# A selective-scan block: where the turned B columns are made, and how two engines' diagonals are placed

## The chip, the cores and the metric

One NeuronCore of a Trainium2 chip runs the whole program. The metric is the device time in microseconds, the median of the runs; lower is better. Engines are named as in the profile: PE (TensorE; PEld is its weight load), DVE (VectorE), ACT (ScalarE), POOL (GpSimd), SP (SyncE, which here only issues DMAs).

## The reference, cut to what matters

The program is two residual layers on a batch of 8 images of 64 x 64 x 96. The change lies in the first one, a two-dimensional selective scan. For each of 8 images and 4 directions k (rows, columns, and both reversed) a sequence of 4096 positions is scanned in 192 channels with 16 states each:

```
dA = jnp.exp(dl[..., None] * A)
h = dA * h + (dl * ul)[..., None] * Bl[:, :, None, :]
y = jnp.einsum('bkdn,bkn->bkd', h, Cl)
```

Before it stand a group norm, a projection, a 3x3 depthwise convolution with SiLU and the projections to delta, B and C; behind it the sum of the four directions, a layer norm, a gate, a projection, and a second layer (an FFT-like upsampling, a squared two-matrix block and a low-pass).

## The kernel before

`scan_phase` is the long stage. A **step** is 1024 positions of one image, one direction and 96 of the 192 channels; there are 256 steps. Two steps (the two channel halves) share B, C and the projections and are called a **chunk** here: 128 chunks. A step has 12 **units**. A unit has 128 partitions (32 channels x 4 states) and 1024 positions; `ORDER = (2,2,2,0,3,3,3,0,1,1,1,0)` gives the group of 4 states of each of the 12 units. This text writes e0 to e11 for the units of a chunk's first step and o0 to o11 for those of its second.

Each unit goes through five engines' in-order lists:

- ACT `exp` (L841): E = exp(A * delta), three buffers (`NE`), so the exponential of a unit waits for the scan three units back. Each place of ACT's list makes the exponential two units ahead.
- PE `fill` (L642 or L677): the drive dl * u * B, spread over the partitions, into one of three PSUM slots (`NP = 3`). Where the group is 0 it is a plain spread of B (L642), multiplied by DVE (L742). In all others it is a product of the turned dl * u (`dluT`) with diagonal matrices of B: for groups 3 and 1 ACT makes these matrices (`diag`, L831, 64 small instructions a chunk), for group 2 (units 0 to 2 of a step) POOL makes them with two `affine_select` (`diagp`, L950). PE fills two units ahead of the unit in hand.
- DVE `scan` (L761): the recurrence, into four buffers H (`NH = 4`), so the scan of a unit waits for POOL's product four units back.
- POOL `weigh` (L961): HC = H * C, six buffers (`NHC`), so the product of a unit waits for the sum of the group of three that ended six units back or less.
- PE `sum_y` (L700, with L690 and L696 ahead of it in some directions): the sum over states, three units at a time in two halves. Its second half for units e6 to e8 stands in PE's list behind the fill of o2, and POOL's product of o0 waits for it.

Side jobs lie between the units: `x` (projection of the next chunk, L627, at e4), `dt` (two delta projections, L636, at e6 and e8; ACT's softplus of them, L807, at e8 and e10), `lt` (the transposes that give `dluT`, L657). On DVE the **split** (L736) stands behind the scan of e6 and waits for ACT's copies of the projection. POOL also makes dl * u (L942), once behind e7 and once behind o1.

Every unit and every side job takes the next of the three PSUM slots in one ring. A slot is free again when the job three places before it in the ring has been read:

```
place_of = {job: i for i, job in enumerate(ring)}
def bank(*job):
    return P[place_of[job] % NP]
```

B's columns must be turned (positions on the partitions) before the diagonals can be made. Before the change this is eight small matmuls (L652) at the head of `lt` of the next chunk, at o1, into spare columns of that job's slot (`BLT_AT`), copied by ACT to `blt` (L816) at o4. POOL's two selects stand behind its products of o5 and o7 (`POOL_AT = (6, 8)`). ACT's 64 diagonals are dealt over its places by `DIAGS`, whose first entry is the place of o3.

Order and names of the directions: k runs 0, 1, 3, 2 in even images and 2, 1, 3, 0 in odd ones. In the last two directions of an image earlier sums are added (L690), in direction 0 the skip term is (L696). Directions 1 and 3 read u in column order.

Of the kernel before, what the change touches and what calls it, by code (L numbers as in the profile page):

```python
# [16 lines left out]
C = 96  # L17
# [17 lines left out]
def namer(nc, ctx, prefix):  # L35

    def sem(name):
        return ctx.enter_context(nc.semaphore(f"{prefix}_{name}"))
    return sem
# [269 lines left out]
def scan_phase(nc, ctx, T, S):  # L309

    sem = namer(nc, ctx, "scan")
    NBLK = TC // 128
# [4 lines left out]
    KIND = tuple(DIRECT if g == GDIRECT else DIAGONAL for g in ORDER)  # L317
    ON = GDIAG + (GPOOL,)
    NDIAG = 4 * len(ON)
    DIAGS = (0, 0, 3, 8, 4, 3, 7, 17, 0, 0, 0, 11, 9, 2, 0, 0, 0, 0, 0, 0, 0, 0, 0, 0)  # L320
    DIAG_AT = 15
    PARTS = 2
    POOL_AT = (6, 8)
    NSLOT = 5
    NDUR = 3
    NP = 3
    BLT_AT = 416
    FILL_AHEAD = 2
    wx = T("wx", [C, NK, 2, 128])
    dtw = T("dtw", [C + NR, NK * ND], F32R)  # L330
# [4 lines left out]
    selt = T("selt", [C, NDIAG], F32R)  # L335
# [18 lines left out]
    blt = T("blt", [128, NBLK * NDIAG])  # L354
# [3 lines left out]
    sx = T("sx", [C + NR, 2, TC], F32R)  # L358
# [15 lines left out]
    NCHUNK = NSTEP // 2  # L374
    NUNIT = 12 * NSTEP
    NACT = 4 * NBLK * len(GDIAG)
# [8 lines left out]
    sx_split = sem("sx_split")  # L385
    dt_done = sem("dt_done")
    dl_made = sem("dl_made")
    dlu_made = sem("dlu_made")
    lt_done = sem("lt_done")
    lt_copied = sem("lt_copied")  # L390
    bt_copied = sem("bt_copied")
    diag_made = sem("diag_made")
    dl_out = [sem(f"dl_out{i}") for i in range(2)]
# [8 lines left out]
    pool_diag_made = sem("pool_diag_made")  # L402
    exp_done = sem("exp_done")
    scan_done = sem("scan_done")
# [36 lines left out]
    def slot(m, j):  # L441
        return (NJ * m + j) % NSLOT

    def loaded(m, j):
        return 64 * ((NJ * m + j) // NSLOT + 1)
# [39 lines left out]
    def side_jobs(n, x):  # L485
        c = n // 2 + 1
        jobs = []
        if n % 2 == 0:
            if x == 1:
                jobs += [("lt", n + 1)]  # L490
            if x == 4 and c < NCHUNK:
                jobs += [("x", c)]
            if x == 6 and c < NCHUNK:
                jobs += [("dt", 2 * c)]
            if x == 8 and c < NCHUNK:
                jobs += [("dt", 2 * c + 1)]
        elif x == 1 and c < NCHUNK:
            jobs += [("lt", 2 * c)]
        return jobs

    ring = [("x", 0), ("dt", 0), ("lt", 0), ("dt", 1)] + [("unit", un) for un in range(FILL_AHEAD)]
    for un in range(NUNIT):
        if un + FILL_AHEAD < NUNIT:
            ring += [("unit", un + FILL_AHEAD)]
        ring += side_jobs(*divmod(un, 12))
    place_of = {job: i for i, job in enumerate(ring)}
    released = {"unit": scan_done, "x": sx_split, "dt": dl_made, "lt": lt_copied}

    def bank(*job):
        return P[place_of[job] % NP]  # L510

    def bank_free(e, *job):
        i = place_of[job] - NP
        if i >= 0:
            e.wait_ge(released[ring[i][0]], ring[i][1] + 1)
# [97 lines left out]
    def tensor(e):  # L613
        def project(c, sub):
            b, k, ci, _ = steps[2 * c]
            t0 = t_of(k, ci) + sub * 512
            if sub == 0:
                bank_free(e, "x", c)
                rows_wait(e, 2 * c)
            o = bank("x", c)[:, sub * 512:(sub + 1) * 512]  # L620
            if k % 2:
                o = o.rearrange("p (w h) -> p h w", h=HW)
            for h in range(2):
                x = u[:, h, t0:t0 + 512]
                if k % 2:
                    x = u[:, h, :].rearrange("p (h w) -> p h w", w=HW)[:, :, t0 // HW:(t0 + 512) // HW]
                r = e.matmul(o, wx[:, k, h, :], x, start=h == 0, stop=h == 1)  # L627
            if sub:
                r.then_inc(x_done)

        def delta(m):
            b, k, ci, half = steps[m]
            bank_free(e, "dt", m)
            e.wait_ge(sx_split, m // 2 + 1)
            for sub in range(2):
                r = e.matmul(bank("dt", m)[0:C, sub * 512:(sub + 1) * 512], dtw[:, k * ND + half * C:k * ND + (half + 1) * C],  # L636
                             sx[:, m // 2 % 2, sub * 512:(sub + 1) * 512], start=True, stop=True)
            r.then_inc(dt_done)

        def spread(o, c):  # L640
# [2 lines left out]
                             start=True, stop=True)  # L643
            return r

        def turn(m):
            o = bank("lt", m)
            bank_free(e, "lt", m)
            if m % 2 == 0:
                e.wait_ge(sx_split, m // 2 + 1)  # L650
                for k in range(NBLK):
                    e.matmul(o[:, BLT_AT + NDIAG * k:BLT_AT + NDIAG * (k + 1)], sx[0:C, m // 2 % 2, k * 128:(k + 1) * 128],  # L652
                             selt[:], start=True, stop=True)
            e.wait_ge(dlu_made, m + 1)
            for k in range(NBLK):
                at = k // 4 * 512 + k % 4 * C
                r = e.transpose(o[:, at:at + C], dlu[:, k * 128:(k + 1) * 128], idn[0:C, 0:C])  # L657
            r.then_inc(lt_done)
# [49 lines left out]
        def side_job(name, n):  # L708
            if name == "x":
                project(n, 0)  # L710
                project(n, 1)
            elif name == "dt":
                delta(n)
            else:
                turn(n)

        side_job("x", 0)
        side_job("dt", 0)
        side_job("lt", 0)
        side_job("dt", 1)  # L720
        for un in range(FILL_AHEAD):
            fill(un)
        for un in range(NUNIT + 12):
            n, x = divmod(un, 12)
# [63 lines left out]
    def scalar(e):  # L788
# [9 lines left out]
        def delta(m):  # L798
            b, k, ci, half = steps[m]
            kk = k * 2 + half  # L800
            e.wait_ge(dt_done, m + 1)
            if m >= 2:
                e.wait_ge(dl_out[m % 2], 16 * (m // 2))
                e.wait_ge(dlu_made, m - 1)
            if m % 2 and m > 3:
                e.wait_ge(y_stored, 16 * (m - 3))
            e.activation(dl[m % 2], bank("dt", m)[0:C, :], ACT.Softplus, bias=dtb[:, kk:kk + 1]).then_inc(dl_made)  # L807

        def turn(m):
            o = bank("lt", m)  # L810
            e.wait_ge(lt_done, m + 1)
            if m % 2 == 0:
                if m:
                    e.wait_ge(diag_made, NACT * (m // 2))
                    e.wait_ge(pool_diag_made, PARTS * (m // 2))
                e.copy(blt[:].rearrange("p (n k) -> p k n", k=NBLK),  # L816
                       o[:, BLT_AT:BLT_AT + NBLK * NDIAG].rearrange("p (k n) -> p k n", n=NDIAG)).then_inc(bt_copied)
            if m >= 2:
                e.wait_ge(fill_done, last_of(m - 2, kinds=(DIAGONAL,)) + 1)
            e.copy(dluT[:, m % 2, :, :].rearrange("p (s k) c -> p s (k c)", s=2),  # L820
                   o.rearrange("p (s x) -> p s x", s=2)[:, :, 0:NBLK // 2 * C]).then_inc(lt_copied)
# [37 lines left out]
        def out_dl(m):  # L859
            if m >= 4:  # L860
                for j in range(NJ):
                    e.wait_ge(dlr_in[slot(m - 4, j)], loaded(m - 4, j))
            e.wait_ge(dl_made, m + 1)
            e.dma_start(S["dl"][m % 4], dl[m % 2]).then_inc(dl_out[m % 2], 16)
# [21 lines left out]
        out_bc(0)  # L886
        delta(0)
        out_dl(0)
        turn(0)
        delta(1)  # L890
        out_dl(1)
        e.wait_ge(a_made, 2)
        made = sum(DIAGS[:24 - DIAG_AT])
        diagonal(0, 0, min(made, 4 * NBLK))
# [3 lines left out]
        for un in range(NUNIT + 12):  # L898
            n, x = divmod(un, 12)
            c = n // 2 + 1  # L900
            exp(un + 2)
            if n < NSTEP and n % 2 == 0 and c < NCHUNK:
                if x == 6:
                    out_bc(c)
                if x == 9:
                    out_dl(2 * c)
                if x == 11:
                    out_dl(2 * c + 1)
            if x == 6 and n:
                store_y(n - 1)  # L910
            if un % 2 == 0 and has_carry(un - 1):
                carry(un - 1)
            if x == 5 and n:
                copy_y(n - 1)
            if n == NSTEP:
                continue
            if n % 2 == 0:
                if x == 2:
                    turn(n + 1)
                if x == 5 and c < NCHUNK:  # L920
                    project(c)
                if x == 8 and c < NCHUNK:
                    delta(2 * c)
                if x == 10 and c < NCHUNK:
                    delta(2 * c + 1)
            elif c < NCHUNK:
                if x == 4:
                    turn(2 * c)
            y = (12 * n + x - DIAG_AT) % 24
            d = c if 12 * (n % 2) + x >= DIAG_AT else c - 1  # L930
            if d < NCHUNK:
                diagonal(d, sum(DIAGS[:y]), DIAGS[y])

    def pool(e):
# [32 lines left out]
        for un in range(NUNIT + 1):  # L967
# [9 lines left out]
            else:  # L977
                if x == 2 and n + 2 < NSTEP:
                    delta(n + 2)
                if x in POOL_AT and c < NCHUNK:  # L980
                    diagonal(c, POOL_AT.index(x))

# [831 lines left out]
```

## Time and profile before

| | |
|---|---|
| median of 3 runs | 11437.5 us (11436.28 to 11439.11) |
| the profiled execution: its own time | 11433.25 us |
| its span, first to last instruction | 11431.5 us |
| stretch of the 128 splits | 624.7 to 9660.6 us |
| busy: PE, DVE, ACT, POOL | 10219.9, 9414.9, 8518.6, 9042.7 us |
| mean granted TensorE clock | 0.96 |

Shares are over the whole span; the scan is some 9100 us of it, and there the four engines are all busy for 82 to 92% of the time. So the shares don't name a bound, and the lists have to be read unit by unit.

### The profile page before, as it was taken

How to read it: one execution, taken by the hardware profiler on the slowest of the kernel's cores; microseconds unless marked ns; L12 is line 12 of the kernel's file. 1: busy time of each engine (PE TensorE's matmuls, PEld its weight loads, DVE VectorE, ACT ScalarE, POOL GpSimd, SP SyncE). 2: the span in 40 equal slices, each digit the busy share in tenths (PEclk: the TensorE clock that was granted, in tenths of full speed). 3: DMA queues.
4: the chain of work that ended last, by engine and by line, in shares of the span. 5: the costliest groups of instructions: out<-in, count | busy, mean ns of one | idle time of the engine just before them, and what ended most of it. 6: DMA issues, size and time to landing. Idle time of an engine off the chain costs nothing. (4 is left out here: it accounts for less than half of the span.)

```text
span 11431.5 us, 430806 instructions
## 1 busy us (share of the span) xinstructions
PE 10219.9 (89%) x185900; PEld 7314.0 (64%) x185900; DVE 9414.9 (82%) x5727; ACT 8518.6 (75%) x15618; POOL 9042.7 (79%) x3978
## 2 busy tenths in 40 slices
PE   8988898889988888899889888998898889799999
PEld 5656666666666666666666666666666666488888
DVE  7868888888888888888888888888888888555554
ACT  3478888888888888888888888888888888355454
POOL 1169999998999999999999999899999999634340
PEclk9989999999999999999999999999999999899999
DMA  3355666566656665666566656665666566322220
GB/s 100 111 156 155 163 168 167 155 163 163 167 156 163 168 163 155 163 167 164 155 163 168 165 156 163 166 166 154 163 171 166 154 164 165 94 70 68 66 68 13
DMA packets 547581, 1653.42 MB, mean 145 GB/s; under 512 B 148562, under 2 KB 149362, under 8 KB 542872
## 3 DMA queue, kind: packets, MB, share of 16 engines
q1 hardware_dynamic: 484248, 1416.10, 48.0%
q10 hardware_dynamic: 61440, 209.76, 6.1%
q8 instruction: 1471, 24.10, 0.9%
q14 instruction: 422, 3.46, 0.1%
HBM read 1251.98 MB, written 373.29 MB: 142 GB/s over the span
## 5 line engine op out<-in xcount | busy, mean ns | idle before, releaser
L961 POOL TENSOR_TENSOR HC<-H,crep 128x1024 f32<-128x1024 f32 x3072 | 7210.9, 2380 | 720.7 <-PE psum L700 681.7
L761 DVE TENSOR_TENSOR_SCAN H<-E,car,psum 128x1024 f32<-128x1024 f32 x2304 | 5282.4, 2334 | 535.7 <-PE psum L677 282.8
L841 ACT ACTIVATE E<-dlr,am 128x1024 f32<-128x1024 f32 x3072 | 3468.7, 1144 | 1335.2 <-DVE H L761 1311.3
L677 PE MATMUL psum<-diag,dluT 128*32 128x128 f32 x98304 | 3225.5, 275 | 360.1 <-DVE H L761 354.4
L677 PEld LDWEIGHTS psum<-diag,dluT 128*32 128x32 f32 x98304 | 2761.2, 110 | 1094.4 <-DVE H L761 702.8
L831 ACT ACTIVATE diag<-idn,blt 128x128 f32<-128x128 f32 x8192 | 2512.4, 389 | 42.5 <-PE psum L677 41.8
L677 PE MATMUL psum<-diagp,dluT 128*32 128x128 f32 x49152 | 1812.7, 302 | 656.8 <-POOL diagp L950 537.0
L677 PEld LDWEIGHTS psum<-diagp,dluT 128*32 128x32 f32 x49152 | 1636.5, 123 | 1027.7 <-issue 826.8
L700 PE MATMUL psum<-HC,sely 128*32 128x512 f32 x12288 | 2152.4, 598 | 22.5 <-POOL HC L961 21.3
L761 DVE TENSOR_TENSOR_SCAN H<-E,psum 128x1024 f32<-128x1024 f32 x768 | 1718.1, 2276 | 227.8 <-PE psum L677 84.9
L742 DVE TENSOR_TENSOR psum<-dur,psum 128x1024 f32<-128x1024 f32 x768 | 929.9, 1211 | 5.1 <-PE psum L642 1.1
L700 PEld LDWEIGHTS psum<-HC,sely 128*32 128x32 f32 x12288 | 431.4, 110 | 409.9 <-issue 365.6
L642 PE MATMUL psum<-sx,selb 96*128 96x512 f32 x1536 | 587.8, 463 | 7.1 <-DVE H L761 7.0
L642 PEld LDWEIGHTS psum<-sx,selb 96*128 96x128 f32 x1536 | 249.7, 189 | 431.8 <-DVE H L761 230.8
L1643 POOL TENSOR_TENSOR y<-y,tmp 96x1024 f32<-96x1024 f32 x60 | 189.6, 3210 | 417.0 <-DMA tmp<-scr_yk 417.0
L950 POOL TENSOR_SCALAR_AFFINE_SELECT diagp<-blt 128x2048 f32<-128x2048 f32 x256 | 514.9, 2012 | 2.0 <-ACT blt L816 2.0
L627 PE MATMUL psum<-u,wx 96*128 96x512 f32 x1024 | 475.7, 607 | 20.2 <-DVE dtw L773 20.2
L942 POOL TENSOR_TENSOR dlu<-dlt,u 96x1024 f32<-96x1024 f32 x128 | 340.0, 2656 | 175.4 <-ACT dlt L807 175.4
L1358 PEld LDWEIGHTS psum<-w2s,hs 128*100 128x100 f32 x4800 | 447.3, 168 | 15.2
L736 DVE TENSOR_TENSOR sx<-psum,sx 38x1024 fp32r<-38x1024 f32 x128 | 157.1, 1228 | 357.4 <-ACT sx L796 357.4
L1358 PE MATMUL psum<-w2s,hs 128*100 128x96 f32 x4800 | 447.8, 252 | 0.0
L45 PE MATMUL psum<-xp,wtap 96*96 96x512 f32 x1728 | 417.0, 400 | 0.0
(140 smaller groups left out, 9403.0 us busy)
## 6 DMA issues: line engine op xcount, KB each, us to landing
dur<-scr_dlu SPq DMA_DIRECT2D x3072, 128.0 KB, 3.5
dlr<-scr_dl SPq DMA_DIRECT2D x3072, 128.0 KB, 4.1
crep<-scr_bc SPq DMA_DIRECT2D x512, 256.0 KB, 4.9
crep<-scr_bc SPq DMA_DIRECT2D x1024, 128.0 KB, 3.0
scr_dlu<-dlu SPq DMA_DIRECT2D x256, 384.0 KB, 3.1
scr_yk<-yt ACTq DMA_DIRECT2D x256, 384.0 KB, 3.1
scr_dl<-dlt ACTq DMA_DIRECT2D x128, 384.0 KB, 4.0
scr_dl<-yt ACTq DMA_DIRECT2D x128, 384.0 KB, 4.6
```

The costliest lines, as they stand in the source:

```text
L45: r = e.matmul(o, w[p], x[q], start=first and i == 0, stop=last and i == 2)
L627: r = e.matmul(o, wx[:, k, h, :], x, start=h == 0, stop=h == 1)
L642: r = e.matmul(o[:, sub * 512:(sub + 1) * 512], selb[:], sx[0:C, c % 2, sub * 512:(sub + 1) * 512], start=True, stop=True)
L677: r = e.matmul(bank("unit", un)[32 * q:32 * q + 32, i * 128:(i + 1) * 128], dluT[:, m % 2, i, 32 * j:32 * j + 32], diagp[:, q, i, :] if g ...
L700: r = e.matmul(yps[32 * j:32 * j + 32, cols], sely[:], HC[:, (3 * i + j) % NHC, cols], start=g == 0 and k != 0 and not second(m), stop=g = ...
L742: e.tensor_tensor(bank("unit", un), dur[:, dur_slot(m, j), :], bank("unit", un), ALU.mult).then_inc(mul_done)
L761: e.tensor_tensor_scan(H[:, un % NH, ::step], decay[:, ::step], drive[:, ::step], init, ALU.mult, ALU.add).then_inc(scan_done)
L831: e.mul(diag[:, blk, 4 * a + q, :], idn[:], blt[:, n:n + 1]).then_inc(diag_made)
L841: e.activation(E[:, un % NE, :], dlr[:, slot(m, j), :], ACT.Exp, scale=am[:, ae:ae + 1]).then_inc(exp_done)
L950: e.affine_select(diagp[:, part * n:(part + 1) * n, :, :].rearrange("p q k t -> p (q k) t"), blt[:, lo:lo + n * NBLK].unsqueeze(2).to_broa ...
L961: e.tensor_tensor(HC[:, un % NHC, :], H[:, un % NH, :], crep[:, g, :], ALU.mult).then_inc(hc_done)
L1358: r = e.matmul(o[0:NU, i * C:(i + 1) * C], hs[:, q % 2, j, i * NU:(i + 1) * NU], w2s[:, j, :], start=j == 0, stop=j == 2)
```

## The change

Four edits, all in `scan_phase`. The eight matmuls that turn B become a side job `bt` with a slot of its own in the ring, issued at e10 (behind the fill of o0), and ACT copies the result at e11. They leave `lt`. POOL's selects go from behind the products of o5 and o7 to behind those of o3 and o5. ACT's diagonals go from heaps of up to 17 at one place to 3 to 6 at each.

```
-    DIAGS = (0, 0, 3, 8, 4, 3, 7, 17, 0, 0, 0, 11, 9, 2, 0, 0, 0, 0, 0, 0, 0, 0, 0, 0)
+    DIAGS = (0, 0, 4, 6, 6, 6, 6, 6, 6, 5, 3, 5, 6, 5, 0, 0, 0, 0, 0, 0, 0, 0, 0, 0)
-    POOL_AT = (6, 8)
+    POOL_AT = (4, 6)
-    BLT_AT = 416
...
             if x == 8 and c < NCHUNK:
                 jobs += [("dt", 2 * c + 1)]
+            if x == 10 and c < NCHUNK:
+                jobs += [("bt", c)]
...
-    released = {"unit": scan_done, "x": sx_split, "dt": dl_made, "lt": lt_copied}
+    released = {"unit": scan_done, "x": sx_split, "dt": dl_made, "bt": bt_copied, "lt": lt_copied}
...
+        def turn_b(c):
+            o = bank("bt", c)
+            bank_free(e, "bt", c)
+            e.wait_ge(sx_split, c + 1)
+            for k in range(NBLK):
+                r = e.matmul(o[:, NDIAG * k:NDIAG * (k + 1)], sx[0:C, c % 2, k * 128:(k + 1) * 128], selt[:], start=True, stop=True)
+            r.then_inc(bt_done)
+
         def turn(m):
             o = bank("lt", m)
             bank_free(e, "lt", m)
-            if m % 2 == 0:
-                e.wait_ge(sx_split, m // 2 + 1)
-                for k in range(NBLK):
-                    e.matmul(o[:, BLT_AT + NDIAG * k:BLT_AT + NDIAG * (k + 1)], sx[0:C, m // 2 % 2, k * 128:(k + 1) * 128],
-                             selt[:], start=True, stop=True)
...
+        def turn_b(c):
+            e.wait_ge(bt_done, c + 1)
+            if c:
+                e.wait_ge(diag_made, NACT * c)
+                e.wait_ge(pool_diag_made, PARTS * c)
+            e.copy(blt[:].rearrange("p (n k) -> p k n", k=NBLK),
+                   bank("bt", c)[:, 0:NBLK * NDIAG].rearrange("p (k n) -> p k n", n=NDIAG)).then_inc(bt_copied)
...
                 if x == 10 and c < NCHUNK:
                     delta(2 * c + 1)
+                if x == 11 and c < NCHUNK:
+                    turn_b(c)
```

The same copy leaves ACT's `turn`. The ring around the new job was `dt e11 o0 o1 o2 o3 lt o4` and is `dt e11 o0 bt o1 o2 o3 lt o4`.

## Rows read from the trace of the kernel before

**Rows 1.** The page: busy us (share of the span) and instructions of each engine.

```profile
PE 10219.9 (89%) x185900; PEld 7314.0 (64%) x185900; DVE 9414.9 (82%) x5727; ACT 8518.6 (75%) x15618; POOL 9042.7 (79%) x3978
```

**Rows 2.** One line's instructions: the splits, one a chunk, first and last start.

```profile
L736 DVE TENSOR_TENSOR sx<-psum,sx x128: 1227/1228/1228, 624.7 to 9660.6; 38x1024 fp32r<-38x1024 f32 x128
```

**Rows 3.** Who waited for POOL's selects (us, times), from their line's answer.

```profile
  PE psum L677: 537.0, 128
```

**Rows 4.** POOL in order of time, direction 3: from o2 on.

```profile
4680.16 14.07 POOL L961 TENSOR_TENSOR HC<-H,crep 128x1024 f32<-128x1024 f32 x6
...
4697.10 9.39 POOL L961 TENSOR_TENSOR HC<-H,crep 128x1024 f32<-128x1024 f32 x4
4706.44 2.01 POOL L950 TENSOR_SCALAR_AFFINE_SELECT diagp<-blt 128x2048 f32<-128x2048 f32 x1
4708.41 4.69 POOL L961 TENSOR_TENSOR HC<-H,crep 128x1024 f32<-128x1024 f32 x2
```

**Rows 5.** DVE in the same stretch: o6; e0; e3's multiply; the next split.

```profile
4699.66 2.29 DVE L761 TENSOR_TENSOR_SCAN H<-E,psum 128x1024 f32<-128x1024 f32 x1 [1.82 <-POOL HC L961]
...
4718.91 2.35 DVE L761 TENSOR_TENSOR_SCAN H<-E,car,psum 128x1024 f32<-128x1024 f32 x1 [2.18 <-PE psum L677]
...
4726.32 1.21 DVE L742 TENSOR_TENSOR psum<-dur,psum 128x1024 f32<-128x1024 f32 x1
...
4740.26 1.23 DVE L736 TENSOR_TENSOR sx<-psum,sx 38x1024 fp32r<-38x1024 f32 x1 [2.67 <-ACT sx L796]
```

**Rows 6.** PE in the same stretch: o1's fill; sum, L652; fills of e0, e1.

```profile
4683.07 1.95 PE L677 MATMUL psum<-diagp,dluT 128*32 128x128 f32 x64 [0.93 <-ACT yt L807]
...
4687.44 1.03 PE L700 MATMUL psum<-HC,sely 128*32 128x512 f32 x6
...
4688.97 0.95 PE L652 MATMUL psum<-selt,sx 96*128 96x12 f32 x8
...
4715.21 6.18 PE L677 MATMUL psum<-diagp,dluT 128*32 128x128 f32 x128 [4.83 <-POOL diagp L950]
```

**Rows 7.** PE in that fill: stretch, us, busy (x), granted clock, DMA share, GB/s.

```profile
4715.00:4720.00 5.00, 4.79 (x92) 0.50 1.04 221
```

**Rows 8.** Direction 0, last of an image: POOL, PE and DVE around e0.

```profile
5065.04 2.03 POOL L950 TENSOR_SCALAR_AFFINE_SELECT diagp<-blt 128x2048 f32<-128x2048 f32 x1
...
5073.85 3.70 PE L677 MATMUL psum<-diagp,dluT 128*32 128x128 f32 x128 [2.20 <-POOL diagp L950]
...
5076.24 7.04 DVE L761 TENSOR_TENSOR_SCAN H<-E,car,psum 128x1024 f32<-128x1024 f32 x3 [0.67 <-POOL HC L961]
...
5083.20 1.21 DVE L742 TENSOR_TENSOR psum<-dur,psum 128x1024 f32<-128x1024 f32 x1
```

**Rows 9.** DVE, four scans without a wait.

```profile
5040.49 9.06 DVE L761 TENSOR_TENSOR_SCAN H<-E,car,psum 128x1024 f32<-128x1024 f32 x4
```

**Rows 10.** First and last of 126 chunks: POOL's first select, DVE's multiply of e3.

```profile
710.43 2.05 POOL L950 TENSOR_SCALAR_AFFINE_SELECT diagp<-blt 128x2048 f32<-128x2048 f32 x1
...
729.55 1.21 DVE L742 TENSOR_TENSOR psum<-dur,psum 128x1024 f32<-128x1024 f32 x1
...
9557.01 2.00 POOL L950 TENSOR_SCALAR_AFFINE_SELECT diagp<-blt 128x2048 f32<-128x2048 f32 x1
...
9575.12 1.21 DVE L742 TENSOR_TENSOR psum<-dur,psum 128x1024 f32<-128x1024 f32 x1
```

**Rows 11.** Direction 2, a late e9: DVE e11's multiply; POOL from e8.

```profile
4114.20 1.21 DVE L742 TENSOR_TENSOR psum<-dur,psum 128x1024 f32<-128x1024 f32 x1
...
4112.46 14.12 POOL L961 TENSOR_TENSOR HC<-H,crep 128x1024 f32<-128x1024 f32 x6
```

**Rows 12.** PE waits with no releaser: the longest of ten above 1.6 us.

```profile
2794.69 0.37 PE L677 MATMUL psum<-diagp,dluT 128*32 128x128 f32 x1 [4.94 <-issue]
```

**Rows 13.** ACT: exponentials of o1, o2 behind the softplus; 17 diagonals.

```profile
4684.33 2.19 ACT L841 ACTIVATE E<-dlr,am 128x1024 f32<-128x1024 f32 x2
...
4711.89 5.07 ACT L831 ACTIVATE diag<-idn,blt 128x128 f32<-128x128 f32 x17
```

More of the change, by code:

```diff
@@ L390, in scan_phase @@
     lt_copied = sem("lt_copied")
+    bt_done = sem("bt_done")
     bt_copied = sem("bt_copied")
@@ L499, in side_jobs @@
         return jobs
-    ring = [("x", 0), ("dt", 0), ("lt", 0), ("dt", 1)] + [("unit", un) for un in range(FILL_AHEAD)]
+    ring = [("x", 0), ("dt", 0), ("bt", 0), ("lt", 0), ("dt", 1)] + [("unit", un) for un in range(FILL_AHEAD)]
     for un in range(NUNIT):
@@ L713, in side_job @@
                 delta(n)
+            elif name == "bt":
+                turn_b(n)
             else:
@@ L718, in tensor @@
         side_job("dt", 0)
+        side_job("bt", 0)
         side_job("lt", 0)
@@ L811, in turn @@
             e.wait_ge(lt_done, m + 1)
[L812 to L817, printed above, removed]
             if m >= 2:
@@ L888, in scalar @@
         out_dl(0)
+        turn_b(0)
         turn(0)
```

## The prediction, made before the changed kernel was run

> **What bounds the kernel now.** The page comes first, to see that it gives no answer: all four engines are busy for most of the time [rows 1]. The line of the splits gives the beat: 127 intervals from 624.7 to 9660.6, 71.15 us each [rows 2]. What DVE must do in one is 24 scans of 2.24, six multiplies of 1.24 and a split of 1.23, 62.4 us; POOL's 24 products of 2.34, two selects and two dl * u come to about 65. Neither fills 71.15, so the beat is a loop through several lists, and the timeline of each engine over one chunk shows it.
>
> In a chunk of direction 3, POOL works without a gap from e8 through its first select at 4706.44 (call this time Z) [rows 4]. Its second select stands two products later, Z + 1.97 + 4.67, and ends at Z + 8.6. PE had run dry 4.83 us before, waiting for just that; then its fills of e0 and e1 take 6.18 for 128 matmuls, against 3.70 elsewhere [rows 6, 8]. The granted clock in that stretch is 0.50, so PE runs at 1.2 instead of 2.4 GHz after having stood idle [rows 7]. The Trainium skill has this rule: TensorE: Matmul & The Clock Gate, What's actually happening, says that the array is throttled by default and activity releases it. By that rule, the trace agrees: the fill behind the idle stretch has 0.50. DVE therefore starts e0 late, after 2.18 idle, and reaches e3's multiply at Z + 19.88 [rows 5]. From there to the next split PE's list sets the pace (fills, sums, the projection), 13.94 us [rows 5], and this tail is within 0.1 us of 13.9 in 119 of the 126 chunks I read. The loop closes: split, delta, POOL's unbroken run, second select, PE's slow fills, DVE, PE's list, split. Every chunk has a wait of PE for the selects, 537.0 us over 128 [rows 3].
>
> What the change can move is thus one distance, from Z (o5 is weighed) to e3's multiply. I read it in 126 chunks, the first 19.12 and the last 18.11 [rows 10]; the mean is 19.75. By kind: 19.82 in directions 1 and 3 (64 chunks); in the two others 19.18 (direction 0, first of an image), 19.23 (2, first), 20.59 (2, last), 19.73 (0, last), 16 chunks each. Direction 0 as the last is unlike the rest: PE has more sums, POOL starts later, and DVE waits for POOL's product of o8, 0.67, and hardly for the fill. Its undisturbed distance is 83.20 - 65.04 = 18.16 [rows 8].
>
> **The selects two places earlier.** POOL's work is the same. The second select now ends at Z + 3.9, before PE gets to e0, so the wait for it and the slow fill go. But o6's product comes behind both selects instead of one. It ends at Z - 4.67 (o3 done) + 1.97 + 4.67 + 1.97 + 2.35 = Z + 6.29, with 2.34 a product from 4697.10 to 4706.44 [rows 4]. DVE's o10 needs its H buffer, and a scan starts 0.21 after the product that frees it: o2's ends at 4697.10 + 2.35 = 4699.45 and o6 starts at 4699.66 [rows 4, 5]. So o10 starts at Z + 6.5. From there nothing else holds DVE: o10 2.24, multiply 1.24, then o11, e0, e1, e2 at (9.06 - 2.35)/3 = 2.24 each, with 0.02 more at a change of operation, 12.5 in all [rows 9]. e3's multiply comes at Z + 19.0. o8's product ends at Z + 11.0 and e0 begins at Z + 12.2, o10's ends at Z + 15.6 and e2 begins at Z + 16.7: POOL is ahead by then. So the gain is 0.84 a chunk in directions 1 and 3, little in the others, 19.75 - 19.0 = 0.75 on average, and direction 0 as the last loses 0.8 in its undisturbed chunks. The stall doesn't vanish, it moves from e0 to o10.
>
> **The new job in the ring.** The eight matmuls are no more than before: 0.95 [rows 6]. Their slot costs more. With `bt` in the ring, o1's fill waits for the scan of e11 instead of the softplus, and o2's for the scan of o0 instead of e11's. In most chunks PE is held by the softplus here (0.93 at o1 [rows 6]); `bt` takes that place and everything behind it shifts by 0.8 to 0.95. PE's list from o1's fill to the end of the second sum is 4687.44 + 1.03 - 4683.07 = 5.4, and about 0.2 later POOL may begin o0 [rows 6]. Today POOL begins o0 at 4680.16 + 9.34 = 4689.5 [rows 4]; with the shift it may at 4683.07 + 0.85 + 5.6 = 4689.5. It just fits in direction 3. POOL is earlier against the split elsewhere: I find 0.15 missing on average over directions 1 and 3, 0.45 and 0.55 in 0 first and 2 last. In direction 2 first, e9 is late in about half the chunks: e11's multiply is at 4114.20, its scan ends at 4117.7, o1's fill begins there, the sum comes at 4123.3, but POOL would begin o0 at 4112.46 + 9.34 = 4121.8 [rows 11], 1.5 late; half of them so and half at 0.6 make 1.0. In 0 last POOL is late anyway, nothing. POOL has no gap up to o6, so each delay goes straight to e3. Weighted mean: (64 x 0.15 + 16 x (0.45 + 0.55 + 1.0 + 0))/128 = 0.33. Bounds: 0 (if `bt` slips between) and 1.5 in all but the last kind, 1.3 on average. I take 0.33, since it is read from the same rows for each kind.
>
> DVE's o2 starts up to 0.9 later by the same shift; it is hidden, because o6 waits for POOL (1.82 [rows 5]). ACT's new wait for `bt_done` has the exponential of o2 behind it: that ended at 4686.5 [rows 13], o2's scan began near 4687.8, and the copy takes a third of a us. Covered by 1 us; uncovered it would cost 0.3 a chunk. B's columns are ready some 10 us ahead of the first select, so POOL doesn't wait for them. Taking the matmuls out of `lt` gives PE 0.8 back at o1; what follows waits for DVE, so it pays nothing.
>
> **ACT's diagonals.** 64 a chunk before and after, 5.07/17 = 0.30 each [rows 13]. A place now holds an exponential (1.05) and six (1.8), 2.9 us, against 2.24 to 3.5 on DVE. Followed place by place from o5, the exponential of e0 is done at Z + 8 and wanted at Z + 12.2, that of e2 at Z + 13.5 and wanted at Z + 16.7. All 64 are done at e4 as before, and group 3's 32 at o10, ahead of e4's fill. ACT has 2 us less at e2 to e4, which frees e6's scan a little; but the split behind it waits for the projection, so it is worth nothing. I cost it at 0; were its 3 us of cover gone, each us late would be 127 us. No DMA moves and no SP wait changes.
>
> **PE's waits without a releaser.** Ten times PE stops for 1.6 to 4.9 us inside these very fills [rows 12], and clusters near the ends of images lift the two last kinds. Together they make about 40 us of the means above. In the new order e1's fill has 3.7 us of room before its scan, so a part is swallowed; I keep half as lost, 20 us (bounds 0 and 40).
>
> **The sum.** Directions 1 and 3: 64 x (19.82 - 18.98 - 0.15) = 44. Direction 0 first: 16 x (19.18 - 18.98 - 0.45) = -4. 2 first: 16 x (19.23 - 18.98 - 1.0) = -12. 2 last: 16 x (20.59 - 18.98 - 0.55) = 17. 0 last: 16 x 0.75 = 12. That is 57, less the 20 kept: 37 us. The profiled execution of 11433.25 (span 11431.5) goes to 11396; the median of the runs is 4 us above it, so 11400 there.
>
> **The rivals.** (a) **The slot costs more, and it is slower.** Place: POOL's o0, waiting for the second sum behind o2's fill. If POOL is 1.5 late in the 112 chunks of rows 11's pattern, that is 168 us lost against the 97 that the selects give without it, less 20: 11437.5 + 91 = 11529; halfway, at a mean of 0.8, about +27, 11465. It decides from a mean delay of 0.6. For it: the margin in direction 3 is nil and PE has no spare time between the softplus and o3. Against: outside direction 2 e11 is early. (b) **The clock falls again.** PE now waits from its fill of e0 to the end of o10, some 3 us, in directions 1 and 3. At half speed a fill is 3.1 instead of 1.85 [rows 6, 8]; e1 and e2 have that room. If it were still slow at e5, e6 and the projection, in the tail of 13.94 that nothing covers, 2 us in every third chunk would be 85 us: 11485. Against: in today's chunks it comes back within the fill. By the rule of the Trainium skill named above (TensorE: Matmul & The Clock Gate) each such wait could end in a slow fill; it gives no time for the tail. (c) **It moves and nothing comes of it**: the wait goes from e0 to o10 and the slot takes the rest, mean delay 0.5 to 0.7: 11420 to 11445. (d) **All of it is found**: no slot cost and no PE stops, 97 + 6: 11335.
>
> **How the numbers follow.** The forecast, a gain of 15 to 75 us, has 0.42; (d) 0.08; (c) 0.23; (a) 0.17; (b) 0.10. About 0.2%, 23 us, is what a measurement of this kernel tells from no change. Faster by more takes (d) and most of the forecast, 0.47; within it (c) and the weak end, 0.26; slower (a) and (b), 0.27. The likeliest case's own range is 11362 to 11422; the range for 8 in 10 reaches to most of (a) and (b) and to (d), 11340 to 11500.
>
> **What would show it.** Right: PE's wait for the selects is nearly gone, e0 has no wait and granted clock near 1 there; DVE waits about 2 us at o10 for POOL's product instead; e3's multiply is 12.5 behind o10's start; the tail stays 13.9. POOL shows short waits for the sum at o0, longest in direction 2 first. Wrong: a POOL gap at o0 above 1 us in directions 1 and 3, exponentials that DVE waits for, a tail longer than 14, or a clock below 1 at e5.

## The result, and the profile after

| | median (lowest to highest), us | ratio to before (95% interval) |
|---|---|---|
| before, 18 runs | 11435.91 (11415.60 to 11445.67) | |
| after, 18 runs | 11462.77 (11452.13 to 11468.12) | 1.0023 (1.0016 to 1.0031) |

The change makes the kernel 27 us slower; a gain of 37 was forecast. The time is inside the range, the sign is wrong. The profiled execution took 11456.9 us (span 11455.2), 23.7 more than the one of before.

The page first, to be read beside [rows 1]: same matmuls and operations, and DVE and POOL busy for as long as before but for 25 us.

```profile
PE 10249.5 (89%) x185900; PEld 7221.2 (63%) x185900; DVE 9439.5 (82%) x5727; ACT 8486.9 (74%) x15618; POOL 9043.0 (79%) x3978
```

The line of the splits, as [rows 2]: (9684.8 - 625.0)/127 = 71.34 us a chunk against 71.15. All of the loss is in the loop.

```profile
L744 DVE TENSOR_TENSOR sx<-psum,sx x128: 1227/1227/1229, 625.0 to 9684.8; 38x1024 fp32r<-38x1024 f32 x128
```

Who waited for POOL's selects, as [rows 3], where it was 537.0 us in 128 waits:

```profile
  PE psum L682: 1.6, 1
```

So PE's wait for the selects is gone, as the change was meant to do, and the kernel is slower all the same. POOL in a chunk of direction 3 (after; start, length, times), as [rows 4]: the selects stand behind o3 and o5, and o6 is the first of the nine products at 4717.38.

```profile
4704.04 4.73 POOL L974 TENSOR_TENSOR HC<-H,crep 128x1024 f32<-128x1024 f32 x2
4708.74 2.00 POOL L963 TENSOR_SCALAR_AFFINE_SELECT diagp<-blt 128x2048 f32<-128x2048 f32 x1
4710.71 4.73 POOL L974 TENSOR_TENSOR HC<-H,crep 128x1024 f32<-128x1024 f32 x2
4715.40 2.00 POOL L963 TENSOR_SCALAR_AFFINE_SELECT diagp<-blt 128x2048 f32<-128x2048 f32 x1
4717.38 21.11 POOL L974 TENSOR_TENSOR HC<-H,crep 128x1024 f32<-128x1024 f32 x9
```

DVE in the same chunk, as [rows 5]: o10; o11, e0... e3's multiply; the split.

```profile
4719.98 2.29 DVE L769 TENSOR_TENSOR_SCAN H<-E,psum 128x1024 f32<-128x1024 f32 x1 [2.05 <-PE psum L682]
...
4732.34 1.21 DVE L750 TENSOR_TENSOR psum<-dur,psum 128x1024 f32<-128x1024 f32 x1
...
4746.28 1.23 DVE L744 TENSOR_TENSOR sx<-psum,sx 38x1024 fp32r<-38x1024 f32 x1 [3.32 <-ACT sx L804]
```

Z, the moment at which o5's product would be done with no select ahead of it, is 4.67 behind the first select's start now: 4713.41. o10 starts at Z + 6.57 (predicted 6.5) after 2.05 idle. The view names PE, but o10's fill had been there: what ended last is o6's product, 4717.38 + 2.35 = 4719.73. e3's multiply comes at Z + 18.93 (predicted 19.0), the tail is 13.94 as before. In this chunk everything runs by the plan. To see where the sum went I read all 126 chunks from the timelines of both kernels, in four distances that add up to the beat. Each number is of one profiled execution of each kernel:

| us over 126 chunks, after minus before | predicted | measured |
|---|---|---|
| split to POOL's first dl * u | 0 | +0.2 |
| from there to Z (the slot of `bt`) | +42 | +76.0 |
| Z to e3's multiply (the selects, PE's stops) | -97 + 20 | -98.2 |
| tail: e3's multiply to the next split | 0 | +47.7 |
| sum | -37 (by kinds, as in the prediction) | +25.7 |

**The tail.** 120 of the 126 tails were below 14.05 us before; 53 are now, and 62 lie between 14.3 and 15, seven above. Here is PE in a chunk with one of 15.88 (direction 1, after): e1's fill, e3's spread, the transposes of `lt`, and e4's fill at 8025.62, whose 64 matmuls take 3.64.

```profile
8015.40 1.95 PE L682 MATMUL psum<-diagp,dluT 128*32 128x128 f32 x64 [2.37 <-DVE H L769]
...
8021.64 0.72 PE L644 MATMUL psum<-sx,selb 96*128 96x512 f32 x2
8023.38 0.88 PE L662 MATMUL psum<-idn,dlu 96*128 96x96 f32 x8 [1.02 <-DVE H L769]
8025.62 3.64 PE L682 MATMUL psum<-diag,dluT 128*32 128x128 f32 x64 [1.36 <-DVE H L769]
```

The windows there (stretch, length, PE busy, PEld, DVE, ACT, POOL, granted clock, DMA share, GB/s): 1.00 up to 8024.00, and 0.50, which is 1.2 GHz, in the fill. The clock's own record has the fall at 8024.62, inside the third wait (8024.26 to 8025.62).

```profile
8010.00:8024.00 14.00, 10.12 (x221) 6.49 (x220) 11.99 (x7) 12.70 (x34) 14.00 (x7) 1.00 0.75 168
8025.00:8031.00 6.00, 5.38 (x80) 3.87 (x83) 5.70 (x4) 6.00 (x16) 6.00 (x3) 0.50 0.97 233
```

Clock and tail go together in every chunk: in all 73 whose tail is above 14.05 the mean granted clock over e4's fill is 0.65 or less, and in the 53 others it is 1.00. In 71 of the 73 the clock falls within about 1 us of the fill's start.

The Trainium skill (TensorE: Matmul & The Clock Gate, What's actually happening) says that the throttled state is the default and that activity releases it. By that rule alone the trace is not explained: PE had worked 10.12 of 14.00 us in the chunk shown and lost the clock all the same, behind waits of 2.37 us and less.

**The slot.** It costs 0.60 a chunk instead of 0.33. Two neighbouring chunks of direction 1 (after) show what of it is the slot itself and what is not. First PE's fills of e9 and e10, `bt`, and POOL's o0, where all goes well:

```profile
3393.37 1.95 PE L682 MATMUL psum<-diag,dluT 128*32 128x128 f32 x64 [2.34 <-DVE H L769]
3395.61 1.95 PE L682 MATMUL psum<-diag,dluT 128*32 128x128 f32 x64 [0.28 <-DVE H L769]
...
3403.13 1.06 PE L653 MATMUL psum<-selt,sx 96*128 96x12 f32 x8 [0.88 <-ACT yt L815]
...
3409.72 4.70 POOL L974 TENSOR_TENSOR HC<-H,crep 128x1024 f32<-128x1024 f32 x2 [0.32 <-PE psum L705]
```

The next chunk has the same first wait, but the fill behind it is slow:

```profile
3464.48 5.31 PE L682 MATMUL psum<-diag,dluT 128*32 128x128 f32 x128 [2.33 <-DVE H L769]
...
3476.26 1.96 PE L682 MATMUL psum<-diagp,dluT 128*32 128x128 f32 x64 [0.56 <-DVE H L769]
...
3481.86 4.70 POOL L974 TENSOR_TENSOR HC<-H,crep 128x1024 f32<-128x1024 f32 x2 [1.37 <-PE psum L705]
```

The two fills take 5.31, e9's scan starts 1.46 late, and o1's fill, which in the new ring waits for the scan of e11, waits 0.56 for it behind `bt`. POOL's o0 waits 1.37 instead of 0.32. Before, o1's fill asked only for the softplus. e11's multiply, a mark of this, stands 12.27 behind the split on average in direction 1, 11.48 before. e9's fill runs at half clock in 20 of the 32 chunks of direction 1 (before: in none) and in 11 of the 16 of direction 2 as the first (before: in 7). In direction 1 POOL's o0 is 1.12 later than before in those 20 chunks and 0.29 in the other 12.

### The profile page after: what moved, and what is told of

The parts are those of the page before. It is cut to its first block and busy times, and to the rows that moved or that the text cites. A ratio compares the mean times of both kernels' runs of the same rounds, so it can differ in the third digit from the quotient of the medians.

```text
span 11455.2 us, 431061 instructions
## 1 busy us (share of the span) xinstructions
PE 10249.5 (89%) x185900; PEld 7221.2 (63%) x185900; DVE 9439.5 (82%) x5727; ACT 8486.9 (74%) x15618; POOL 9043.0 (79%) x3978
## 5 line engine op out<-in xcount | busy, mean ns | idle before, releaser
L682 PE MATMUL psum<-diag,dluT 128*32 128x128 f32 x98304 | 3381.3, 283 | 501.6 <-DVE H L769 499.2
L682 PEld LDWEIGHTS psum<-diag,dluT 128*32 128x32 f32 x98304 | 2900.6, 114 | 1225.0 <-DVE H L769 806.0
L841 ACT ACTIVATE diag<-idn,blt 128x128 f32<-128x128 f32 x8192 | 2549.9, 389 | 47.1 <-PE psum L682 46.3
L705 PE MATMUL psum<-HC,sely 128*32 128x512 f32 x12288 | 2184.8, 607 | 70.6 <-POOL HC L974 68.9
L682 PE MATMUL psum<-diagp,dluT 128*32 128x128 f32 x49152 | 1644.2, 278 | 311.7 <-DVE H L769 294.5
L682 PEld LDWEIGHTS psum<-diagp,dluT 128*32 128x32 f32 x49152 | 1385.9, 112 | 709.7 <-DVE H L769 563.8
L803 ACT COPY dlt<-psum 32x1024 f32<-32x1024 f32 x128 | 128.7, 1005 | 454.0 <-PE psum L629 454.0
```

The lines of the kernel that those rows point to most:

```text
L682: r = e.matmul(bank("unit", un)[32 * q:32 * q + 32, i * 128:(i + 1) * 128], dluT[:, m % 2, i, 32 * j:32 * j + 32], diagp[:, q, i, :] if g ...
L705: r = e.matmul(yps[32 * j:32 * j + 32, cols], sely[:], HC[:, (3 * i + j) % NHC, cols], start=g == 0 and k != 0 and not second(m), stop=g = ...
L841: e.mul(diag[:, blk, 4 * a + q, :], idn[:], blt[:, n:n + 1]).then_inc(diag_made)
```

## The experiments

Times are medians with five rounds beside runs of the kernel before; "slot", "e3" and "tail" are the sums of the table above for that kernel, us over 126 chunks against before. Three kernels take the parts of the change one at a time.

**The selects alone.** Before with

```
-    POOL_AT = (6, 8)
+    POOL_AT = (4, 6)
```

> Kernel before with one edit: the two selects behind the products of o3 and o5. Theory A (the slot of bt costs about 0.6 us a chunk at POOL's o0, the earlier selects give about 0.78 a chunk, and a fall of the clock at e4's fill takes 0.38 of it back): no slot cost here, so the distance from o5 weighed to e3's multiply falls by some 98 us in all, the tail grows by some 40: 11436 - 55 = about 11380, ratio 0.995. Rival B (the earlier selects are themselves worth nothing, since the wait only moves from e0 to o10 and the clock takes the rest): within 0.2% of the kernel before, 11415 to 11460.

11389.44 against 11434.63, ratio 0.9961 (0.9949 to 0.9974). Slot +0.1, e3 -97.6, tail +47.9: the tail's loss belongs to the selects, not to the new slot. Half of what they gain is given back. e11's multiply in direction 1 is at 12.25 here, as in the whole change, and without the slot it costs nothing.

**The slot alone.** After with the old `POOL_AT` and `DIAGS`.

> Kernel after with the selects back behind o5 and o7 and the old dealing of ACT's diagonals: only bt with its own slot is left. Theory A: POOL's o0 is late by 0.6 us a chunk on average and nothing hides it, so 76 us more than before: about 11510, ratio 1.0066; the wait of PE for the selects is there as before and the tail stays 13.9. Rival B (the slot costs nothing by itself, the loss comes from the earlier selects and the clock): within 0.2% of before.

11487.4, ratio 1.0049 (1.0036 to 1.0061). Slot +59.5, e3 -4.2, tail -2.5. e11's multiply in direction 1 is at 11.44.

**The diagonals alone.** Before with the new `DIAGS`.

> Kernel before with the new dealing of ACT's 64 diagonals alone. Theory A: nothing, 11436 within 0.2%; DVE's short wait for ACT's carry ahead of e6 shrinks, and the split behind it still waits for the projection. Rival C (the even dealing makes exponentials late and is part of the loss): slower by 20 to 40 us, with DVE waiting for E between o8 and e3.

11428.99, ratio 0.9996 (0.9987 to 1.0006), -2.4 in the loop. No change, as costed. The three sums make -49.4 + 52.9 - 2.4 = +1.1 against +25.7 for the whole, so 25 us belong to no part alone. Of these, 15 are in the slot's distance: the selects make e9's fill late (e1, in 31 chunks), and only the slot makes POOL wait for it (e2 has the slot and the late fill in one chunk). The other 10 are 4 in the e3 distance and 6 in the tail; what they come from is not shown, and the diagonals alone move the tail by 4 without a change of the time.

**PE kept at work.** If the tail's loss is the clock alone, matmuls that nothing reads, placed in PE's waits, must give it back. After with

```
+        def warm(n):
+            for _ in range(n):
+                e.matmul(yps[C:128, 0:128], sely[:], idn[:], start=True, stop=True)
...
+            if n % 2 and x == 10:
+                warm(9)
+            if n % 2 == 0 and x == 1:
+                warm(4)
...
+            if n % 2 == 0 and x == 1:
+                warm(5)
```

These are nine behind e0's fill, and four ahead of and five behind the transposes of `lt`.

> Kernel after with extra small matmuls that nothing reads, 9 behind e0's fill, 4 ahead of and 5 behind the transposes at e1, written to the 32 unused partitions of the y slot: they fill part of PE's waits. Theory A (the tail is longer because the clock is at half when e4 is filled): granted clock 1.0 in that fill, the tail back to 13.9, some 45 us less than after, about 11418. Rival D (the tail is longer for another reason, such as the fill of e4 waiting for something, or traffic): no gain, or a loss where the extra matmuls push e4's fill back.

11418.33, ratio 0.9988 (0.9979 to 0.9997). Slot +80.2, e3 -91.9, tail +0.8; 118 of 126 tails are below 14.05. PE at e4's fill (L715 are the added matmuls, each counted as two), and its window there, granted clock 1.00:

```profile
4714.12 1.06 PE L715 MATMUL psum<-idn,sely 128*32 128x128 f32 x8
4715.21 0.88 PE L662 MATMUL psum<-idn,dlu 96*128 96x96 f32 x8
4716.02 1.28 PE L715 MATMUL psum<-idn,sely 128*32 128x128 f32 x10
4717.45 1.96 PE L682 MATMUL psum<-diag,dluT 128*32 128x128 f32 x64
```

```profile
4717.00:4723.00 6.00, 5.15 (x142) 3.86 (x143) 5.96 (x4) 6.00 (x17) 6.00 (x3) 1.00 0.88 219
```

That the clock is the cause of the tail's loss is shown from both sides: in the changed kernel each long tail goes with half clock at e4's fill and no short one does; with these matmuls the clock is 1.00 over every fill of e4, and the loss is gone. The slot's extra is still there, with e11's multiply at 12.51 in direction 1.

**The same for e9's fill.** e4's kernel with nine more in directions 1 and 2 of an image's first half:

```
+            if n % 2 == 0 and x == 6 and not second(n) and steps[n][1]:
+                warm(9)
```

> The changed kernel with small matmuls that nothing reads at four places: 9 behind e0's fill, 4 and 5 around the transposes at e1, and, new against the earlier one with three places, 9 ahead of e9's fill in directions 1 and 2 as the first of an image. Theory A (part of what the slot costs there is the clock again: e9's fill at half clock makes e11 late, and o1's fill now waits for e11's scan): e11's multiply is back at 11.4 behind the split in all of them, the delay of POOL's o0 falls from 80 to about 55 us in all, and the time from 11418 to about 11390. Rival (e9's lateness has another cause): 11418 within 0.2%.

11397.65 against 11432.87, ratio 0.9970 (0.9959 to 0.9981). Slot +51.9, e3 -92.7, tail +3.3, sum -37.4; e11 is back at 11.44. So of the slot's 76 to 80 us, 28 are e9's fills at half clock, and 52 are the slot at full clock. With the clock held, the whole change gives the -37 that was forecast, though of other terms: slot 52 instead of 42, e3 16 better, tail +3. That the sums agree is luck.

**The slot's matmuls twice.** Is it PE's time that the slot costs, or only the waiting order? The slot alone (e2), with the eight issued twice:

```
-            for k in range(NBLK):
+            for k in list(range(NBLK)) * 2:
```

> The kernel with bt in its own slot as the only edit, its eight matmuls issued twice. Theory G (the slot costs because PE's list from the softplus to the second sum has no room, so each 0.8 us of bt goes to POOL's o0): the delay grows by up to 0.8 a chunk in all kinds but direction 0 as the last, some 85 us: 11487 + 85 = 11570. Rival H (it costs because o2's fill now waits for the scan of o0, not for PE's time): no change, 11487 within 0.2%.

11687.58, ratio 1.0225 (1.0209 to 1.0240); slot +255.1 instead of +59.5. That is PE's time and more: 195.6/126 = 1.55 a chunk for eight more matmuls, which take 0.89 (PE and one window, e7's kernel):

```profile
4857.45 1.95 PE L653 MATMUL psum<-selt,sx 96*128 96x12 f32 x16 [0.88 <-ACT yt L815]
4859.33 2.55 PE L682 MATMUL psum<-diagp,dluT 128*32 128x128 f32 x64
...
4866.61 4.71 POOL L974 TENSOR_TENSOR HC<-H,crep 128x1024 f32<-128x1024 f32 x2 [2.77 <-PE psum L705]
```

```profile
4861.00:4863.00 2.00, 2.00 (x26) 1.04 (x19) 1.07 (x1) 1.17 (x3) 2.00 (x2) 0.50 0.96 260
```

o1's fill takes 2.55 instead of 1.95 and the sums behind it are slow too: the clock fell to 0.50 at 4860.53, while PE had instructions without a gap from `bt` on. o1's fill runs at half clock in 57 of the 126 chunks here and in none of e2. Leaving out direction 0 as the last, where the slot costs nothing, POOL's o0 is 2.97 later than before in those 57 chunks and 1.54 in the other 55; in e2 it is 0.53. So the second eight cost 1.0 where the clock holds, which is PE's time for them, and 2.4 where it falls. The first eight cost less than the 0.9 that they take: PE's list between the softplus and POOL's o0 has some 0.4 of room and no more. So the rival that only the waiting order matters is out: eight more matmuls in the same order cost more. Whether the order has a part in the first 0.53 is not shown.

**A place between.** The selects at (4, 6) make o10 wait and PE wait for it; at (6, 8) e0 waits for them. The remaining choice is one place ahead, without the slot:

```
-    POOL_AT = (6, 8)
+    POOL_AT = (5, 7)
```

> Kernel before with the selects behind the products of o4 and o6. Theory A (e3's multiply comes 12.4 behind the scan of o10 when two selects stand ahead of o6's product; with one ahead of it, o10 starts 2 us earlier and e3 is held by o10's product instead, as in the undisturbed chunks of direction 0, 18.1 behind Z): the distance falls from 19.75 to 18.1, 208 us in all; the tail grows by at most the 48 us seen with the selects behind o3 and o5: 11225 to 11275, likely 11250, ratio 0.984. Rival E (what held e3 was PE's clock only, so that any place that ends the wait gives the same): as with the selects behind o3 and o5, 11389.

11291.16 against 11429.43, ratio 0.9877 (0.9860 to 0.9893). e3 -160.8 (mean 18.48), tail +24.4. The gain is real and 40 us less than expected. The tail was allowed for; what is short is the e3 distance, 161 where 208 were expected. PE still waits for the second select, but DVE doesn't wait for it: its wait at e0 adds up to 1.0 us over 126 chunks (before: 231). PE and DVE in one chunk:

```profile
4651.74 3.70 PE L677 MATMUL psum<-diagp,dluT 128*32 128x128 f32 x128 [1.68 <-POOL diagp L950]
...
4656.46 7.04 DVE L761 TENSOR_TENSOR_SCAN H<-E,car,psum 128x1024 f32<-128x1024 f32 x3
```

The shortfall lies in PE's stops without a releaser [rows 12]. Of those above 1 us there are 27 in the scan here, against 13 before. In the 25 chunks with one near Z or between Z and e3's multiply, the mean distance is 19.86; in the other 101 it is 18.14, the 18.1 expected. Together the stops take 43 us. Why this order has more of them is not known. One of them:

```profile
3958.40 0.85 PE L677 MATMUL psum<-diagp,dluT 128*32 128x128 f32 x10 [5.35 <-issue]
```

Three kernels add unread matmuls to it. **Four and five around the transposes of `lt`:**

```
+            if n % 2 == 0 and x == 1:
+                warm(4)
...
+            if n % 2 == 0 and x == 1:
+                warm(5)
```

> The same (selects behind o4 and o6) with 4 and 5 small matmuls that nothing reads around the transposes at e1. Theory A (the clock falls in the waits ahead of e4's fill): the tail is 13.95 on average, and the time is that of the kernel without them less what its tail has above 13.95, up to 48 us. Rival F (with the selects here PE's waits are shorter and the clock doesn't fall there): the two are equal within 0.2%.

11298.33, ratio 0.9883 (0.9868 to 0.9898), tail +20.4: no gain over e5, though the clock was kept. e5 has 43 tails above 14.05 and half clock at e4's fill in 37 of them; here it is 25 and one. The others are long for another reason, which no run settles; 15 of the 20 us are in direction 0 and direction 2 as the last of an image. **Eight more ahead of e0's fill, nine ahead of e9's as above:**

> As the kernel with selects behind o4 and o6 and small matmuls at e1, with 8 more ahead of e0's fill and, in directions 1 and 2 as the first of an image, 9 ahead of e9's fill. Theory A: e9's fill is no longer at half clock, so the late e9 (e11's multiply 12.6 behind the split instead of 11.5) is gone; in the kernels without bt's slot POOL's o0 has room, so it gives only 0 to 15 us. If e0's fill is held up by the extra matmuls it loses up to 50 us.

11274.28, ratio 0.9863 (0.9849 to 0.9878); e3 -173.6, tail +18.5. **None of the `lt` and e0 ones in direction 0 as the last of an image**, where PE has more sums:

```
-            if n % 2 == 0 and x == 1:
+            if n % 2 == 0 and x == 1 and (steps[n][1] or not second(n)):
...
-            if n % 2 and x == 9:
+            if n % 2 and x == 9 and (steps[n][1] or not second(n)):
```

> Selects behind o4 and o6 with small matmuls ahead of e0's fill, around the transposes at e1 and ahead of e9's fill, as before, but none of the first two kinds in direction 0 as the last, where PE has no wait to fill: 0 to 15 us faster than 11274.

11268.33 against 11432.87, ratio 0.9857 (0.9843 to 0.9870); e3 -176.9, tail +12.7. It is the fastest version measured and beats both kernels; nearly all of it is the one number in `POOL_AT`, and its interval overlaps with those of e5, e6 and e8.

**The kernel before with its clock kept.** Fourteen unread matmuls ahead of e0's fill, selects at their old places:

```
+            if n % 2 and x == 9 and (steps[n][1] or not second(n)):
+                warm(14)
```

> The kernel before, nothing moved, with 14 small matmuls that nothing reads ahead of e0's fill in all kinds but direction 0 as the last: PE still waits for the second select, but isn't idle all the while. Theory A (of the 2.2 us for which DVE waits at e0 most is the half clock of the two fills, the rest the wait for the select): e0 is then held by POOL's product of o8, e3's multiply comes 18.1 to 18.5 behind Z instead of 19.75, and the time is 11230 to 11290. Rival (the late select itself is what holds e0, as the wait's releaser says): at most 30 us faster than before.

11339.93, ratio 0.9920 (0.9906 to 0.9933); e3 -94.5, tail +1.1. That is less than expected, and more than its rival allowed. The clock still falls at e0's or e1's fill in 48 of 126 chunks (before: 112), as in the chunk shown (5.37 for 128):

```profile
4814.48 2.78 PE L710 MATMUL psum<-idn,sely 128*32 128x128 f32 x24
4819.70 5.37 PE L677 MATMUL psum<-diagp,dluT 128*32 128x128 f32 x128 [2.43 <-POOL diagp L956]
```

In direction 1 e3's multiply comes 18.12 behind Z in the median of the 11 chunks that keep the clock there, and 19.08 in the 21 that lose it; before it was 19.72, with the clock lost in all 32. So it is the half clock that made the late select dear, more than the wait itself. Besides, PE stops without a releaser 24 times here (above 1 us), against 13 before. Still, matmuls that compute nothing gain 93 us, as much as the selects gained at their distance, and don't give it back. This is also the fair measure of e9: with such matmuls in both, the whole change is 58 us slower than the order before (11397.65 against 11339.93).

## Why the prediction was wrong

- **The loop and the bound: right.** All of the difference is in the loop named, and the distance that the selects were to shorten is the one that they shortened.
- **The selects' new places: right.** o10 at Z + 6.57 (6.5), e3 at 18.97 on average (19.0), 98 us (97). The stall moved from e0 to o10 as described. What e10 adds is that nearly the same gain at this distance, 94.5, is had without moving the selects, by keeping the clock at e0's and e1's fills.
- **"The tail stays 13.9", costed at nothing: the step that failed.** It is rival (b)'s mechanism in another size: not 2 us in every third chunk, but about 0.6 in half of them and 2 in seven, 47.7 us. I took a wait of PE as spent where the next scan had room. But o10's stall makes PE wait three times on end (2.4, 1.0, 1.4), and the clock falls at the third or just behind it, at the start of the stretch that has no room. With the tail as predicted the kernel would have been faster, -22 instead of +25.7. e1 shows that the selects bring it, the match of long tails and half clock in 73 of 73 chunks and e4 that the clock is how.
- **The slot, +42: right in kind, mis-sized.** 52 at full clock (e9), 76 in the kernel. The missing 24 are e9's fill at half clock, foreseen for half of direction 2 alone (2 first +18.0 of 16 foreseen); it came in direction 1 as well, +26.0 in 32 chunks where 5 were foreseen. e2, with the slot alone, costs 59.5, so some 16 of the 24 are the meeting of two parts: early selects bring the late fill (e11's multiply at 12.25 in e1 and 11.44 in e2), the slot makes it count. What in the new order costs e9's fill the clock, behind the same wait of 2.3 at which it kept it in the chunk before, is not settled.
- **Half of PE's stops kept as lost, 20 us: too much, and in part luck.** The e3 term came out whole (-98). Above 1 us the scan has five such stops in this execution against 13 before, and the chunks with one are in sum 3 us above the median distance, against 25. In e4 and e9, with the same order, there are 13 and 8 stops, and it is 9 us in each. So the new order swallows more of them than half; how many there are differs from kernel to kernel, and no run shows why.
- **ACT's diagonals at nothing: right** (e3). In 8000 us of the scan DVE waited 4.7 us in 3 waits for an exponential by the view of waits.
- **The chances.** Rival (a) was to decide from a mean slot cost of 0.6. It came to 0.60, but with 98 us on the other side that alone would still be faster; it took the slot's and the clock's term together to turn the sign, a case in which two rivals held at once and which I had given no chance of its own.

## What to carry to other kernels

A stall that is moved to a place with room is not free if the engine behind it has a clock that follows its work: follow PE's waits, all of them together, up to the next stretch that nothing covers, and price that stretch at half clock too. Measure beside it the old order with the clock kept: here that alone gave 0.8%, more than the change could. When a wait must be somewhere, try the places between: one place ahead gave 1.2%, two gave 0.4%. And a job added in front of a full list costs its own time for every chunk, so a measurement with the job doubled is a cheap way to see whether there is room.

## What the runs showed of the hardware

- The granted clock fell in the last of three waits of 2.4, 1.0 and 1.4 us; in the 14 us just ahead of that wait PE had worked 10.1. The same three waits stand in the chunk of direction 3 shown first (PE, after), and there e4's fill took 1.95. The same pattern gives either result: e4's fill is slow in 73 of 126 chunks and at full clock in 53.

```profile
4722.32 1.95 PE L682 MATMUL psum<-diagp,dluT 128*32 128x128 f32 x64 [2.38 <-DVE H L769]
...
4730.24 0.88 PE L662 MATMUL psum<-idn,dlu 96*128 96x96 f32 x8 [1.01 <-DVE H L769]
4732.48 1.95 PE L682 MATMUL psum<-diag,dluT 128*32 128x128 f32 x64 [1.36 <-DVE H L769]
```

- It also fell while PE worked: in e7 there is a wait of 0.88, then sixteen matmuls of 12 columns in 1.95 us, then the fall 1.2 us into o1's fill. With sixteen this fill is at half clock in 57 of 126 chunks, with eight (e2) in none.
- Matmuls with 32 output rows in a spare corner of PSUM, never read, keep it up: 18 a chunk (e4), and nine more in 48 of the chunks (e9), raised the mean granted clock from 0.97 to 0.987 (e4) and 0.993 (e9), and 11462.77 to 11397.65 us. They took PE's busy time from 10249.5 to 10652.5 us, and it was faster.
- PE stops inside its small matmuls with no releaser in the trace, up to 5.35 us. Above 1 us there are 13 such stops in the scan of the kernel before, 5 in the changed one and 27 in e5.
